# Graph block with mixture of experts on one core: 42 of the 100 scatters of destination terms go behind the last row gather, ahead of the block border, and router batches are used four tiles sooner

## The reference, cut to what matters

```python
edge_index = jnp.stack([src, dst])
xn = _layernorm(x, axis=-1)
x = x + _L0_gnn_ref(xn, edge_index, ...) + _L0_mix_ref(xn[None], ...)[0]
x = x + _L0_ffn_ref(_layernorm(x, axis=-1)[None], ...)[0]
# in _L0_ffn_ref: the router's attention over its own edges, per head
h = (x_flat @ W_gat).reshape(M, HEADS, NUM_EXPERTS)
a_src, a_dst = (h * att_src).sum(-1), (h * att_dst).sum(-1)
e = jax.nn.leaky_relu(a_src[src] + a_dst[dst], negative_slope=0.2)
ee = jnp.exp(e - e_max[dst])          # e_max, denom: per destination
alpha = ee / (denom[dst] + 1e-16)
agg = jax.ops.segment_sum(h[src] * alpha[:, :, None], dst, ...) + b_gat
# scores -> layer norm, mean over heads, top 2 of 4, softmax; then
for ei in range(NUM_EXPERTS):
    hh = jax.nn.gelu(x @ W1[ei] + b1[ei], approximate=False)
    out = out + g[..., None] * (hh @ W2[ei] + b2[ei])
```

## Time and profile before

| | us |
|---|---|
| median of 3 runs | 4135.55 (4126.72 to 4138.9) |
| the profiled execution | 4134.59 |
| its span, first to last instruction | 4132.8 |
| PE busy | 3223.6 (78%) |
| POOL busy | 2856.3 (69%) |
| DVE busy | 2084.5 (50%) |
| ACT busy | 801.7 (19%) |
| mean granted TensorE clock | 0.906 |

### The profile page before, as it was taken

One profiled execution on the slowest core, in us unless ns is written; L12 is line 12 of the kernel. 1 busy time (PEld: TensorE's weight loads), 2 busy tenths in 40 slices (PEclk: granted clock), 3 DMA queues, 4 the chain that ended last, 5 costly groups with the idle time before them and its releaser, 6 DMA issues. The chain is left out here.

```text
span 4132.8 us, 46229 instructions
## 1 busy us (share of the span) xinstructions
PE 3223.6 (78%) x12938; PEld 2165.0 (52%) x12938; DVE 2084.5 (50%) x4892; ACT 801.7 (19%) x1966; POOL 2856.3 (69%) x2937
## 2 busy tenths in 40 slices
PE   0599899998987888887887799999899999991000
PEld 0355556665655655555555466666666666661000
DVE  6577777776765866665554212223222322312888
ACT  6122222222200111111111122222122221220000
POOL 2677777777777777777775577777777777775610
PEclk6799999999998999999998899999999999995555
DMA  8555555554545666667666222222222222223787
GB/s 260 177 134 134 133 134 135 135 136 132 137 135 137 174 175 173 175 172 202 175 174 157 62 71 64 60 69 77 64 64 58 74 69 66 63 55 92 214 259 256
DMA packets 381412, 540.56 MB, mean 131 GB/s; under 512 B 120314, under 2 KB 297818, under 8 KB 381143
## 3 DMA queue, kind: packets, MB, share of 16 engines
q0 software_dynamic: 119136, 234.44, 25.0%
q1 hardware_dynamic: 243119, 288.12, 21.7%
q10 hardware_dynamic: 19016, 16.48, 1.2%
HBM read 392.03 MB, written 146.74 MB: 130 GB/s over the span
## 5 line engine op out<-in xcount | busy, mean ns | idle before, releaser
L787 POOL DMA_INDIRECT rows<-xn_rows,gsrc x1664 | 1611.1, 968 | 509.8 <-issue 509.2
L1357 POOL DMA_INDIRECT nb<-route_rows,idx x1024 | 1015.9, 992 | 321.8 <-issue 303.1
L1088 PE MATMUL PS<-rows,oh 128*128 128x257 f32 x3328 | 876.0, 412 | 264.6 <-DMA rows<-xn_rows,gsrc 263.2
L1088 PEld LDWEIGHTS PS<-rows,oh 128*128 128x128 f32 x3328 | 646.2, 203 | 412.2 <-DMA rows<-xn_rows,gsrc 303.6
L1690 PE MATMUL PS<-arena,hid 128*125 128x256 f32 x3200 | 700.5, 381 | 29.2 <-ACT hid L1649 20.9
L1682 PE MATMUL PS<-x2g,arena 128*128 128x500 f32 x1600 | 680.1, 586 | 23.5 <-DMA x2g<-x_turned 13.4
L1690 PEld LDWEIGHTS PS<-arena,hid 128*125 128x125 f32 x3200 | 601.0, 188 | 138.8 <-issue 33.1
L1621 DVE TENSOR_TENSOR y_sb<-PS,b_b 125x512 f32<-125x512 f32 x200 | 128.5, 684 | 1041.0 <-PE PS L1690 1040.9
L1682 PEld LDWEIGHTS PS<-x2g,arena 128*128 128x128 f32 x1600 | 305.8, 191 | 383.5 <-issue 357.7
L1649 ACT ACTIVATE hid<-PS,b_sb 128x500 f32<-128x500 f32 x400 | 270.5, 677 | 673.0 <-PE PS L1682 672.8
L824 DVE TENSOR_TENSOR oh<-PS,rel 128x1024 f32<-128x1024 f32 x208 | 253.9, 1221 | 9.2 <-issue 1.0
(11 more groups left out here) (304 smaller groups left out, 3083.9 us busy)
## 6 DMA issues: line engine op xcount, KB each, us to landing
y_rows<-y_sb SPq DMA_DIRECT2D x100, 512.0 KB, 2.7
arena<-y_rows SPq DMA_DIRECT2D x100, 512.0 KB, 5.7
rows<-xn_rows,gsrc POOLq DMA_INDIRECT x1664, 3.4
nb<-route_rows,idx POOLq DMA_INDIRECT x1024, 2.4
sum_rows<-kept SPq DMA_DIRECT2D x104, 128.5 KB
x_rows<-x SPq DMA_DIRECT2D x100, 128.0 KB, 4.7
hid<-x_rows SPq DMA_DIRECT2D x100, 128.0 KB, 6.8
m_in<-sum_rows SPq DMA_DIRECT2D x100, 125.5 KB
```

The source lines that it names most:

```text
L787: pool.indirect_dma_start(out=rows[w][h][:, q, 0:D], out_offset=None, in_=xn_rows, in_offset=bass.IndirectOffsetOnAxis(ap=gsrc[:, s * HU + ...
L1088: last = mm(SUM[:, 0:D + 1], oh[w][h][:, q, :], rows[w][h][:, q, :], start=h == 0 and q == 0, stop=h == 1 and q == HU - 1)
L1357: pool.indirect_dma_start(out=nb[b % NBUF][:, c, :], out_offset=None, in_=route_rows, in_offset=bass.IndirectOffsetOnAxis(ap=idx[:, b * W ...
```

## The change

POOL's list in the graph block gets two waits and 42 of the 100 scatters behind its last row gather: a wait for `s_adz` (the zeros that SP wrote into `ad_rows` at the start of that block) and one for `s_hc` at 43, that is, for the router rows of tiles 0 to 41. The expert block scatters tiles 42 to 99 only. SP's wait for `s_ads` at 1600 is as before. `unit_after` becomes 6 (b + 1) + 3, rounded in the same way.

```diff
+SOONER = 42
 def unit_after(b):
 
-    t = int((b + 1) * 5.8) + 7
+    t = 6 * (b + 1) + 3
     return t if t % 4 < 2 else t + 4 - t % 4
...
                         pool.indirect_dma_start(out=rows[w][h][:, q, 0:D], out_offset=None, in_=xn_rows,
                                                 in_offset=bass.IndirectOffsetOnAxis(ap=gsrc[:, s * HU + q:s * HU + q + 1], axis=0)
                                                 ).then_inc(s_rows[w][(h * HU + q) // QUAD], 16)
+                pool.wait_ge(s_adz, RH * 16)
+                pool.wait_ge(s_hc, SOONER + 1)
+                for t in range(SOONER):
+                    pool.indirect_dma_start(out=ad_rows, out_offset=bass.IndirectOffsetOnAxis(ap=start_i[:, t:t + 1], axis=0),
+                                            in_=ad_all[:, t, :], in_offset=None).then_inc(s_ads, 16)
...
-                for t in range(NT):
+                for t in range(SOONER, NT):
                     pool.indirect_dma_start(out=ad_rows, out_offset=bass.IndirectOffsetOnAxis(ap=start_i[:, t:t + 1], axis=0),
                                             in_=ad_all[:, t, :], in_offset=None).then_inc(s_ads, 16)
```

## The result

The changed kernel takes 4080.61 us (median of 4 runs, 4080.18 to 4080.87). The kernel before, on the same chips, takes 4131.14 us (4126.29 to 4138.9). The ratio is 0.9876 with a 95% interval of 0.9857 to 0.9894: 50.5 us less. The two profiled executions differ by 54.4 us (4134.59 and 4080.18). The forecast was 4082, that is 53.6 us less than the 4135.55 known then. The gain of the medians is 3 us smaller than that, and the kernel before came out 4.4 us faster with a fourth run, so that 4082 lies so close to 4080.61 is in part luck.

What follows compares the result with a forecast made beforehand. POOL was taken as the bound, TensorE with DVE 40 us behind. From the profiled 4134.59 us, -53.5 -2.7 +1.7 +0.9 = -53.6 gave 4081.0; the median lying 1.0 higher, 4082 was predicted, range 4074 to 4096.

Steps and rivals of the forecast that it cites:

- The bound: From block border to last gather POOL is the bound, with TensorE and DVE next, 40 us behind it.
- Part 1: Ahead of the border: 42 scatters fit into POOL's idle 57.8 us and take 53.5 us off the path.
- with 3.9 us to spare before POOL's present release: At the border: the moved scatters end at 2301.5, 3.9 us before POOL is let go at 2305.41.
- Rival (b): At the border: scatters slowed beside DVE's work spill over by 33.8 us, gain shrinks to 20, 4116 us; chance 0.05.
- The term of 0.9 us for the tile pipeline: Graph block: DMA time of 42 scatters is 1.8 us, in the tile pipeline's way between none and all; middle taken.
- Rival (c): Graph block: scatters hold up the tile pipeline, border 92 us later, 4174 us; chance 0.02.
- Part 2: Expert block: DVE waits for no batch but perhaps the late one; 24.6 us of TensorE stalls go, counted as nothing.
- Part 3: End of the gathers: final loads no longer slow POOL's issue, -2.7 us, but the last gather lands slower, +1.7 us.
- The slower landing (+1.7): Last gather, issued 3.2 us behind the final loads' start, lands in 4.0 us instead of 2.3.
- The loads issued until then are nearly through: Late batch: its records are stored at about 3733, when the final loads issued until then are nearly through.
- rival (a): Expert block: batches land some 10 us later than reckoned, TensorE and DVE become the bound, 4095 us; chance 0.08.
- the marks that were to show it: Signs expected in the changed profile, from POOL's idle time of about 4 us at the border to an unchanged 359 us rest.

Runs made afterwards that it cites:

- part 2 alone: Kernel before with only the new, sooner tiles of use, all 100 scatters still behind the border: 4139.6 us against 4133.7, ratio 1.0007.
- landed: Changed kernel plus a POOL wait for the landing of the 42 scatters and a marking memset: span ends 1832.9 us behind the last row gather, against 1830.9.
- e1: Changed kernel with the old tiles of use, so only the 42 scatters moved: median 4086.8 us, the kernel before beside it 4133.7.
- before_store_first: Kernel before with the late batch's record store put ahead of the eight tiles' final loads: 4131.5 us against 4131.4, ratio 1.0005.
- late_loads: Changed kernel with the first eight tiles' final loads behind the late records' store and the repair scatter's landing: median 4076.9 us, ratio to the kernel before 0.9867.
- split_loads: Changed kernel with four tiles' final loads ahead of the late records' store, four behind the repair scatter's landing: median 4078.1 us, ratio to the kernel before 0.9874.
- n38: Changed kernel with 38 scatters ahead of the border instead of 42: 4088.6 and 4084.5 us.
- store_first: Changed kernel with the late batch's record store put ahead of the eight tiles' final loads: median 4080.9 us.

## Why the prediction was right, point by point

**The bound.** POOL was and is the bound; part 2 alone moved TensorE's end by 16.6 us from the border and the kernel's by 1.1. Right.

**Part 1, -53.5 us.** 42 scatters did leave the path, at 1.275 us each. The first neighbour gather came 51.5 us sooner from the last row gather (188.2 to 136.7), since the border moved by 2.0. The failed step is "with 3.9 us to spare before POOL's present release": the release is not the moment by which POOL has to be done. POOL takes 6.04 us from its last instruction to the next block (landed, and the same 6.04 in the changed kernel and five other traces), where DVE takes 2.46. The number I should have compared with 57.8 was 53.5 + 6.0. Rival (b), a spill over the border, thus came true by 2.0 us against the kernel before, by another mechanism than the one I gave it: the scatters themselves kept their 0.97 us. Against the tile pipeline of the same execution POOL was later still, by 4.3 us (6.8 behind DVE's last copy instead of 2.46); 2.4 us of this stayed hidden because the pipeline happened to end sooner, 53.9 us behind the last row gather instead of 56.3.

**The term of 0.9 us for the tile pipeline.** It is too small to be seen: the pipeline's end lies between 50.0 and 56.3 us behind the last row gather in three traces without the scatters, and between 49.6 and 56.6 in nine with them. Rival (c), 92 us, did not come. The Trainium skill, "DMA: Bandwidth & Descriptors" (Specifications), gives a read-modify-write for writes under 512 bytes; no cost of it to the work beside the scatters stands out of this spread.

**Part 2, no wait for a batch, both stalls gone.** Right. The last eviction ended at 3711.1; 3708.8 was predicted, and the border was 2.8 us later. It began 1401.6 us behind the border instead of 1426.7, that is 25.1 us sooner, for 24.6 us of stalls. The part of them that was not idle time went with the granted clock, which was at 0.50, the lower of its two levels (1.2 GHz), behind both stalls (2946.5 to 2952.1 and 3444.3 to 3450.4) and 1.00 from 2952 to 3430; TensorE had been idle for 10.15 and 8.33 us just ahead of them. But as e1 shows, the batches would have been in time at the old tiles as well.

**Part 3, -2.7 +1.7 us.** The sum was right only by accident. The loads' slowing of POOL is worth 3.1 to 3.5 us (before_store_first). The stream became shorter by more than that, 1328.4 us instead of 1336.4. Where the 8.0 us lie can be added up roughly from the two traces. The idle time between gathers, over 0.305 us each, fell from 9.7 to 6.7 us (5.3 in before_store_first). What gathers took above 0.945 us each fell from 6.3 to 0.5 us beside DVE's scans of `m_run` and from 35.0 to 32.8 beside its scans of `rec`, and rose from 7.9 to 10.5 elsewhere. Kernels with the scatters moved have 48.8 to 52.2 us of extra time, of it 0.1 to 2.7 beside the `m_run` scans; those without have 54.5 to 59.9, of it 4.8 to 6.3. Why fewer gathers were held up there was not tested and stays open. The slower landing (+1.7) did not come: the loads began at 3714, 1.6 us behind the last gather instead of 3 us ahead of it, and it landed in 2.4 us.

**The missing term.** "The loads issued until then are nearly through" failed. From the last gather to the first weighing it took 58.6 us instead of 55.0 (3826.25 - 3771.26), 3.6 more: the store of the late records at 3728.70 met the final loads and landed in 8.3 us instead of 3.2. Before, that store was not on the chain: POOL's repair scatter waited 5.04 us for DVE's own work behind it. So of the 5.1 us more some 1.4 lay beside this work, and 3.6 were paid. late_loads and split_loads, which keep the loads out of its way, give 4 us back by their traces.

**The sum.** -51.5 (scatters less border), -8.0 (stream), +3.6 (late records and repair), +0.6 (combining, 306.6 to 307.2) are -55.2 before rounding, and this execution's last row gather was 0.8 us later: -54.4, for -53.6 predicted. Terms were off by 2.0 us (the border), 5.3 (the stream), 1.7 (the landing) and 3.6 (the late records), with both signs, and cancelled. That the sum came within 1 us is luck; that scatters worth 53.5 us left the path is not. The range was set by rival (a) at one end and by the spread of three runs at the other, and held.

Of the marks that were to show it, these were missed: POOL's idle time of about 4 us ahead of the border (6.04), the border within 2 us of 2305.4 (2.8) and the first gather at 2381 (2384.2), for the one reason above; the late batch begun at about 3719 behind a wait of about 10 us (3715.11, 4.0 us), since the stream was shorter and the last gather landed sooner; and the rest of 359 us behind it (363.3), by the missing term. No wait for another batch, groups of 55.5 to 55.6 us throughout and the last eviction came as said.

## What to carry to other kernels

Idle time of an engine ahead of a block border is worth filling with its own later work, if that engine is the bound behind the border; reckon the time it needs to leave the block, which here was 6 us for GpSimd and was longer than the margin. A table that says when results are used only has to come behind their landing; moving it sooner gave nothing that could be measured here, and without the faster producer it delayed the consumer's neighbours. When the bound moves forward, look at what was timed to fall behind it: here prefetches that used to run beside idle waiting came to run beside the one store that everything waits for, and holding them back until the chain of small transfers was over gave 4 us in two traces, while the medians (2.7 and 3.9 us less) do not tell it from noise.

## What the runs showed of the hardware

- POOL needs 6.04 us from the end of its last instruction in a block to its next instruction in the following one, whether indirect DMAs have just been issued or have landed (6.37 once, with 46 scatters); with POOL early, as in the kernel before and n38, the border comes 2.46 us after the start of DVE's last copy.
- A POOL scatter of 128 rows of 16 bytes costs 1.275 us of POOL like a gather of rows of 1 KB with 1.25, and landed 1.2 us after POOL was done with it (landed). No effect on the work beside it stands out of the spread of 7 us in the pipeline's end.
- 5.2 MB of loads queued on the DMA engines delayed the small transfers on the chain: 768 KB stored from SBUF took 3.2 us with no load near it (before, n38, late_loads, split_loads), 3.9 with the loads issued right behind it (store_first), and 8.3 to 9.9 behind them; a gather of 128 records took 2.4 to 2.7 us and 4.2; a scatter of 128 records 2.2, and 5.4 to 6.2.
- POOL's gathers were longer beside DVE's scans: single ones took up to 4.1 us instead of 0.94, and beside the scans of `rec` the 1024 gathers took 31.3 to 36.0 us more in all. A batch of 64 gathers took 2.2 to 4.2 us over its 80 us, before and after, the first and the last batch aside. The Trainium skill, "SBUF — State Buffer" (Who interferes with whom), says that the two engines share a port pair, and that with DVE in a two-port mode whoever issues first has it for the whole instruction while the other fully blocks; a scan is not among the instructions that it lists. Gathers held up for up to 3 us look like such blocking, but no run here shows that the ports are its cause.
- The same 1664 row gathers, in kernels that are alike up to there, took between 1608.8 and 1620.3 us of POOL in twelve executions.
